# A gated attention kernel whose 264 steps run in an order written out by hand: another order, with the same instructions

## The reference

```
x = x + tanh(g_x) * xattn(layernorm(x), ctx, ctx)
x = x + tanh(g_f) * ffn(layernorm(x))
xattn: f_q, f_k, f_v = layer_norm(t) @ w_in.T, 8 heads of 128
       mixed = cw * cos(f_q, f_k) + vw * cos * decorr_scale + ww * q_ratio x k_ratio
       out = (mixed @ f_v) @ w_out.T + b_out
ffn:   q, k, v = x @ Wq, x @ Wk, x @ Wv, 16 heads of 16
       attn[key, query] = softmax over the queries of (q . k) / 16; z[query] = sum over keys of attn * v
       z = l2norm(z @ Wo); z = l2norm(z @ Wff); gelu(z)
```

## Time and profile before

| | us |
|---|---|
| three runs, median | 1335.22 (1333.38 to 1335.81) |
| profiled execution, own time | 1331.52 |
| its span, first to last instruction | 1329.8 |
| PE busy | 1197.1 (90%) |
| DVE busy | 1116.6 (84%) |
| ACT busy | 1012.5 (76%) |
| POOL busy | 206.9 (16%) |

### The profile page before, as it was taken

The page is one execution under the profiler, slowest core; times in us unless marked ns, Lnnn a source line. Parts: engine busy times, 40 slices in busy tenths (PEclk is TensorE's granted clock), DMA queues, the critical chain, the costliest instruction groups (busy, mean ns, idle before and its releaser), DMA issues. The chain is left out here.

```text
span 1329.8 us, 34850 instructions
## 1 busy us (share of the span) xinstructions
PE 1197.1 (90%) x10386; PEld 744.4 (56%) x10386; DVE 1116.6 (84%) x3180; ACT 1012.5 (76%) x3333; POOL 206.9 (16%) x160
## 2 busy tenths in 40 slices
PE   4999967999999999999989899989898999898965
PEld 2677536565646464656565656565555656564531
DVE  5986546798989898989898898989898989898964
ACT  5667113487979797979797979797888888888887
POOL 1443101202020202011110202020202020202000
PEclk9999879999999999999999999999999999999987
DMA  8450024463627281818181818182727254544650
GB/s 257 136 166 20 3 53 80 132 124 111 158 92 176 74 194 50 218 47 220 45 204 51 204 52 208 42 213 52 200 68 194 74 182 85 170 98 142 112 159 17
DMA packets 247888, 162.30 MB, mean 122 GB/s; under 512 B 94538, under 2 KB 235559, under 8 KB 247848
## 3 DMA queue, kind: packets, MB, share of 16 engines
q1 hardware_dynamic: 247848, 161.80, 46.3%
HBM read 86.74 MB, written 42.58 MB: 97 GB/s over the span
## 5 line engine op out<-in xcount | busy, mean ns | idle before, releaser
L1529 ACT ACTIVATE prob<-score,nm 128x256 f32<-128x256 f32 x1024 | 474.9, 485 | 61.4 <-DVE nm L1722 34.0
L1722 DVE TENSOR_REDUCE nm<-score 128x2 f32<-128x512 f32 x512 | 337.3, 681 | 17.2 <-PE score L1433 16.0
L1529 ACT ACTIVATION_READ_ACCUMULATOR prob<-score,nm 128x1 f32 x1024 | 222.5, 217 | 0.0
L1444 PE MATMUL attended<-prob,vsp 128*32 128x256 f32 x2048 | 134.9, 392 | 8.5 <-DVE vsp L1737 7.6
L1433 PE MATMUL score<-qstack,kstack 64*128 64x256 f16 x1024 | 97.0, 277 | 38.6 <-DMA kstack<-parts 27.4
L1642 DVE BATCH_NORM_STATS2 qst<-work 128x6 f32<-128x128 f32 x512 | 112.0, 284 | 22.3 <-PE work L895 22.3
L1588 POOL TENSOR_TENSOR l2r<-l2v,mhalf 128x4 f32<-128x4 f32 x16 | 16.1, 1009 | 599.0 <-DVE l2v L1694 599.0
L893 PE MATMUL work<-wTh,xTh 128*128 128x512 f16 x256 | 98.3, 384 | 5.4 <-DVE xTl L1636 3.5
L894 PE MATMUL work<-wTl,xTh 128*128 128x512 f16 x256 | 98.0, 383 | 0.0
L895 PE MATMUL work<-wTh,xTl 128*128 128x512 f16 x256 | 97.8, 382 | 0.0
L893 PE MATMUL work<-Vph,mTh 128*128 128x256 f16 (+1 forms) x320 | 87.4, 273 | 5.7 <-issue 4.8
(11 more groups left out here) (326 smaller groups left out, 3244.3 us busy)
## 6 DMA issues: line engine op xcount, KB each, us to landing
qstack<-parts SPq DMA_DIRECT2D x64, 256.0 KB, 3.8
kstack<-parts SPq DMA_DIRECT2D x64, 256.0 KB, 4.3
sqE<-sq_rows SPq DMA_DIRECT2D x64, 154.0 KB
s_xin<-in_x SPq DMA_DIRECT2D x8, 1024.0 KB, 6.0
xin<-in_x SPq DMA_DIRECT2D x16, 512.0 KB, 4.2
x2S<-in_x SPq DMA_DIRECT2D x16, 512.0 KB, 3.6
parts<-qh SPq DMA_DIRECT2D x32, 256.0 KB, 2.5
parts<-ql SPq DMA_DIRECT2D x32, 256.0 KB, 2.7
```

The source lines that it names most:

```text
L1444: last = nc.tensor.matmul(pvb[32 * j:32 * j + 32, t, :], vsp[:, k, (4 * e + j) * 2 * FD:(4 * e + j + 1) * 2 * FD], prob[:, n % PG, e, j, : ...
L1529: nc.scalar.activation(prob[:, g % PG, e, j + jj, :], sc[n % SC][:, jj * NQ:(jj + 1) * NQ], ACT.Exp, bias=nm[:, u + jj:u + jj + 1], accum_ ...
L1722: nc.vector.tensor_reduce(nm[:, u:u + 2], sc[n % SC][:, :].rearrange("p (u q) -> p u q", q=NQ), AX.X, ALU.max, negate=True).then_inc(max_r ...
```

## The change

All steps keep their instructions. `ORDER`, `HEAD`, `TAIL` and `MOVED` are replaced; the loop, the steps' code and the number of turns stay. The list of a turn begins elsewhere: `a0`, `a1`, `aux`, `qs2`, `rk`, `G1.h`, `G1.l`, `X1` and `M2` now stand at the end of the turn ahead of the one in which they stood, `back1` and `back2` with them. The bank of each chunk follows from its new place. In the order after, y0 is place 19 of the chunks (counted from 0), d5 place 16.

```diff
 ORDER = """
-G0 X1 G1.h M2 G2.l G0.h qs2 G3 G3.h ldx S2 M3 G1.l G0.l G3.l a0 X2 a0.v res V3 V5 pv1 V3.h M4 V5.h aux back1 M5 V3.l
-V0 X3 rk X4 V5.l z back2 pv1.v R0 S3 V4 V0.h fk0 V4.h X5 P0 M6 S4 X6 M7 V0.l V4.l fk0.h X7 sqe0 V2 M8 sqe1 fk0.l M9
-V2.h fk1 V2.l R1 X8 X9 S5 fk1.h vt1 a1 d0 M10 M11 X10 fk1.l vt0 S6 M12 a1.h P1 a1.l fk2 X11 d0.o E0 S7 fk2.h m0.h M13
-d1 L0 d2 R2 P2 X12 fk2.l M14 m0.l M15 X13 X14 d3 X15 d1.o d2.o S8 m1.h M16 d4 R3 m2.h M17 S9 m1.l X16 m2.l d3.o wq ldy
-d5 X17 d4.o P3 E1 S10 zT0 M18 m3.h zT0.h m4.h M19 y0 X18 m3.l m4.l X19 d5.o m5.h M20 zT1 zT0.f zT1.h L1 m5.l M21 zT0.l
-S11 y0.o M22 y1 X20 zT1.f M23 R4 zT1.l y1.o X21 X22 ln1 O0 X23 R5 back3 O1 q0 S12 S13 P4 O0. P5 lpow q0.o M24 M25 M26
-O1. M27 q1 q2 ln2 q1.o q3 X24 q2.o q3.o zz0 X25 X26 X27 S14 S15 M28 zz1 zz0.h zz0.l E2 zz1.h q4 X28 M29 q5 zz1.l q4.o
-M30 pk0 X29 X30 q6 q5.o M31 X31 pq0 pk0.h L2 R6 pq0.h R7 pk0.l P6 q6.o P7 q7 pq0.l E3 L3 O2 q7.o O2. O3 G5 qs1 pq1 O3.
-G5.h G5.l F1 F2 parts0 pq1.h V1 V1.h back0 pk1 S0 pq1.l G4 V1.l F3 M0 pk1.h pk1.l G4.h G4.l G1 M1 parts1 X0 F4 pv0
-pv0.v qpow G2 S1 G2.h out
+a1.l ldx pv1 V2 pv1.v M3 G4.l V2.h S2 sqe0 M4 M5 X2 V4 V4.h V5 V2.l G3 V4.l sqe1 V5.h V5.l X3 G3.h S3 R0 M6 G0 G3.l X4
+M7 G0.h X5 V3 G0.l fk1 S4 X6 z M8 X7 P0 fk1.h R1 d0 fk1.l P1 M9 S5 V3.h X8 V3.l V0 d0.o M10 X9 m0.h S6 M11 fk2 M12 E0
+V0.h fk2.h m0.l V0.l X10 X11 d1 fk2.l d1.o wq d2 X12 M13 d2.o L0 S7 m1.h R2 M14 X13 d3 vt0 fk0 X14 m1.l m2.h M15 d4
+vt1 S8 d3.o fk0.h m2.l X15 res m3.h M16 R3 P2 d5 X16 P3 M17 X17 fk0.l zT0 m3.l d4.o d5.o zT0.h S9 m4.h S10 M18 E1 m5.h
+m4.l L1 M19 m5.l back3 zT1 ldy zT0.f X18 y0 X19 M20 zT0.l zT1.h M21 zT1.f S11 X20 y1 X21 M22 M23 zT1.l X22 y0.o R4 O0
+X23 y1.o ln1 O1 O0. S12 R5 S13 O1. M24 P4 lpow P5 q0 q1 X24 E2 M25 M26 ln2 q2 q0.o zz0 X25 M27 X26 q1.o S14 X27 S15
+zz0.h zz1 q2.o q3 zz1.h M28 zz0.l zz1.l q4 R6 M29 X28 pq0 q3.o X29 M30 q4.o pk0 pq0.h M31 pq0.l pq1 X30 L2 q5 pk0.h P6
+pk0.l X31 R7 pq1.h P7 q5.o q6 E3 pq1.l q7 L3 O2 q6.o parts0 O3 rk q7.o pk1 O2. O3. V1 qs1 pk1.h G2 pk1.l F1 F2 V1.h
+back0 G2.h V1.l S0 pv0 G2.l F3 pv0.v G5 back2 G1 S1 M0 qpow parts1 M1 G1.h G5.h back1 G4 G5.l G1.l qs2 a0 X0 a0.v a1
+a1.h F4 aux G4.h M2 out X1
 """.split()
 
 HEAD = """
-ldx fk0 fk1 fk0.h fk1.h +ldy fk1.l z fk2 fk2.h fk2.l zT0 zT0.h zT1 zT0.f zT0.l zT1.h fk0.l zT1.f zT1.l q0 q1 q2 q0.o
+fk1 ldx fk1.h fk0 fk1.l z fk2 fk2.h fk0.h fk0.l zT0 zT0.h zT0.f zT1 fk2.l zT1.h zT0.l zT1.f zT1.l q0 q1 q0.o rk q1.o
...
 TAIL = """
...
-X30 E2 X31 pk0.h L2 R7 pq0.h P6 pk0.l pq0.l P7 E3 L3 O2 parts0 O2. O3 back0 O3. pq1 pk1 pq1.h pq1.l F1 pk1.h F2 S0 F3
+P5 S15 M29 zz0.h zz1.h E2 zz0.l zz1.l L2 M30 X28 X29 X30 pq0 M31 R6 X31 pq0.h R7 pk0 pq0.l P6 P7 pk0.h pq1 pk0.l E3 L3
+pq1.h O2 pq1.l parts0 O3 O2. O3. F1 pk1 back0 S0 pk1.h pk1.l parts1 F2 M0 F3 F4 S1 X0 back2 pv0 M1 back1 pv0.v out M2
...
-MOVED = {step: n for n, steps in {0: "G1 G2 G2.h G4 G4.h G4.l G5 G5.h G5.l V1 V1.h V1.l qpow qs1", 1: "M0 M1 S0 S1 X0", 2: "back1 back2 back3 pv1 pv1.v res"}.items() for step in steps.split()}
+MOVED = {step: n for n, steps in {0: "G1 G1.h G1.l G2 G2.h G2.l G4 G4.h G5 G5.h G5.l V1 V1.h V1.l a0 a0.v a1 a1.h aux qpow qs1 qs2 rk", 1: "M0 M1 M2 S0 S1 X0 X1", 2: "back3 pv1 pv1.v res"}.items() for step in steps.split()}
```

More of the change, by code:

```diff
@@ L965 @@
[L965 to L969, removed]
@@ L970 @@
-+q1.o +lpow +q2 +ln2 +q3 +zz0 +zz0.h +q2.o +q3.o +zz0.l +zz1 +q4 +zz1.h +zz1.l +q5 +q4.o +pk0 +q5.o +pq0 +pk0.h +pq0.h
-+q6 +pk0.l +pq0.l +q6.o +q7 +q7.o +pq1 +pq1.h +parts0 +G5 +back0 +pq1.l +G5.h +G4 +V1 +V1.h +G5.l +qs1 +qpow +G4.h
-+pk1 +G4.l +G2 +pk1.h +S0 +V1.l +G2.h +pk1.l +pv0 +M0 +X0 +parts1 +S1 +M1 +G1 +pv0.v
+fk1 ldx fk1.h fk0 fk1.l z fk2 fk2.h fk0.h fk0.l zT0 zT0.h zT0.f zT1 fk2.l zT1.h zT0.l zT1.f zT1.l q0 q1 q0.o rk q1.o
+q2 q2.o q3 q3.o q4 q4.o q5 q5.o q6 q7 V1 q6.o q7.o qs1 V1.h G2 G2.h V1.l G2.l qpow +ldx G5 G1 G1.h G5.h G5.l G1.l G4
@@ new lines @@
+a1 a1.h G4.h qs2 a0 a0.v +a1.l aux +V2 +V2.h +G4.l +V4 +V2.l +V5 +V4.h +G3 +V4.l +G0 +V5.h +G3.h +G0.h +G0.l +G3.l
++V5.l +fk1 +d0 +z +wq +sqe0 +V3 +sqe1 +fk1.h +V3.h +V3.l +V0 +d0.o +m0.h +m0.l +fk1.l +V0.h +V0.l +d1 +fk2 +d2 +fk2.h
++fk2.l +d1.o +m1.h +d2.o +d3 +m2.h +fk0 +fk0.h +d4 +m1.l +m2.l +vt1 +d3.o +m3.h +fk0.l +d5 +zT0 +d4.o +m3.l +zT0.h
++d5.o +m4.h +zT0.f +zT1 +zT0.l +vt0 +zT1.h +ldy +zT1.f +m5.h +y0 +m4.l +m5.l +y1 +zT1.l +y0.o +y1.o +q0 +ln1 +lpow
++q0.o +q1 +q2 +q1.o +ln2 +q2.o +zz0 +zz0.h +zz1 +zz1.h +q3 +zz0.l +zz1.l +q3.o +q4 +pq0 +q4.o +pk0 +pq0.h +pk0.h
@@ L973 @@
++pq0.l +rk +pq1 +pk0.l +pq1.h +q5 +pq1.l +parts0 +back0 +q6 +q5.o +q7 +q6.o +G2 +q7.o +pk1 +pk1.h +V1 +V1.h +qs1 +G2.h
++G2.l +G1 +G1.h +V1.l +S0 +pk1.l +back2 +G5 +parts1 +S1 +G1.l +M0 +qpow +G5.h +X0 +a1 +G5.l +qs2 +pv0 +M1 +a0 +pv0.v
++a1.h +G4 +a0.v +aux +X1 +M2 +back1 +G4.h
 """.split()
 TAIL = """
-qs2 G2.l G0 G1.h back2 X1 G0.h G3 G3.h G1.l M2 M3 a0 a0.v S2 G0.l V3 G3.l V5 pv1 M4 X2 X3 V3.h V3.l aux M5 V5.h X4 V0
-V5.l S3 pv1.v V4 V0.h back1 R0 rk M6 V0.l res X5 S4 M7 V4.h X6 X7 P0 V4.l V2 sqe0 a1 V2.h M8 M9 X8 V2.l R1 S5 d0 sqe1
@@ L982 @@
[L982 to L986, removed]
+res pv1 a1.l pv1.v V2 S2 V2.h M3 sqe0 G4.l V4 M4 V2.l G3 V5 X2 X3 M5 V4.h S3 X4 R0 P0 V4.l G0 V5.h M6 sqe1 G3.h X5
@@ new lines @@
+V5.l S4 V3 X6 G0.h G3.l M7 X7 V3.h M8 ldy M9 G0.l X8 R1 S5 M10 X9 d0 V3.l M11 X10 d0.o S6 V0 d1 m0.h X11 P1 M12 S7 M13
+m0.l R2 V0.h V0.l E0 d1.o d2 wq d3 X12 m1.h M14 X13 S8 d2.o m1.l L0 M15 P2 d4 d3.o X14 m2.h M16 M17 X15 R3 m3.h m2.l
+d5 vt1 X16 vt0 m3.l P3 X17 E1 S9 d4.o m4.h d5.o S10 M18 y0 X18 back3 m5.h M19 M20 M21 X19 m4.l X20 X21 L1 S11 m5.l R4
+M22 y1 X22 S12 M23 y0.o X23 O0 P4 y1.o M24 ln1 O0. lpow M25 X24 O1 S13 M26 O1. X25 ln2 X26 S14 zz0 M27 X27 R5 zz1 M28
+P5 S15 M29 zz0.h zz1.h E2 zz0.l zz1.l L2 M30 X28 X29 X30 pq0 M31 R6 X31 pq0.h R7 pk0 pq0.l P6 P7 pk0.h pq1 pk0.l E3 L3
@@ new lines @@
+pq1.h O2 pq1.l parts0 O3 O2. O3. F1 pk1 back0 S0 pk1.h pk1.l parts1 F2 M0 F3 F4 S1 X0 back2 pv0 M1 back1 pv0.v out M2
+X1 +M3 +pv1 +S2 +M4 +X2 +X3 +pv1.v +M5 +S3 +M6 +R0 +M7 +X4 +P0 +X5 +X6 +S4 +X7 +M8 +M9 +S5 +R1 +X8 +M10 +X9 +X10 +M11
++P1 +S6 +M12 +E0 +M13 +L0 +X11 +S7 +R2 +X12 +P2 +X13 +S8 +M14 +M15 +X14 +M16 +M17 +X15 +S9 +R3 +X16 +M18 +M19 +X17
++X18 +P3 +S10 +M20 +X19 +res +S11 +X20 +E1 +M21 +R4 +M22 +M23 +L1 +back3 +X21 +S12 +X22 +P4 +M24 +X23 +X24 +S13 +M25
++X25 +M26 +O0 +S14 +R5 +M27 +M28 +M29 +X26 +X27 +P5 +E2 +S15 +M30 +L2 +X28 +R6 +X29 +O1 +X30 +M31 +X31 +R7 +P6 +O0.
@@ L987 @@
++P7 +E3 +L3 +O2 +O1. +O2. +O3 +O3. +F1 +F2 +F3 +F4 +out
 """.split()
-MOVED = {step: n for n, steps in {0: "G1 G2 G2.h G4 G4.h G4.l G5 G5.h G5.l V1 V1.h V1.l qpow qs1", 1: "M0 M1 S0 S1 X0", 2: "back1 back2 back3 pv1 pv1.v res"}.items() for step in steps.split()}
+MOVED = {step: n for n, steps in {0: "G1 G1.h G1.l G2 G2.h G2.l G4 G4.h G5 G5.h G5.l V1 V1.h V1.l a0 a0.v a1 a1.h aux qpow qs1 qs2 rk", 1: "M0 M1 M2 S0 S1 X0 X1", 2: "back3 pv1 pv1.v res"}.items() for step in steps.split()}
 CHUNKS = [s for s in ORDER if any(t.startswith(s + ".") for t in ORDER)]
```

## The result

The median of four runs is **1348.04 us** (1347.02 to 1349.10), beside 1334.56 for the kernel before on the same chip: the ratio is 1.0101, 95% interval 1.0083 to 1.0118. The change makes the kernel slower by 13.5 us, 1%. The profiled execution took 1348.43 us with a span of 1346.7, 16.9 more than the profiled one of the kernel before. The two profiles lie further apart than the medians because the profiled execution before, 1331.52 us, was faster than each of the four timed ones (1333.38 to 1335.81), while the one after lies at its median.

The account below looks back on a forecast made before the run. The loop was taken as near TensorE's and VectorE's limits, losing time mostly at the seam. 8.45 + 27.3 + 0.1 + 32.4, plus 1.2 and 0.2, gave 69.6 us a turn, +13 us in fourteen: 1348 us, range 1324 to 1372.

Parts of the forecast that it names:

- The 3.7 us added from the profile before to the median before: Last step of the total: the runs' median lies 3.7 us above the profiled execution, so 1344.5 became 1348 us.
- Transfers: At the seam of two turns: S0's wait under 1 us, z's gone; worth at most some 2.5 us a turn.
- The chain of 8.45 us over GpSimd: At the seam, O3., nrs, rq: qs2 can start 8.45 us after TensorE leaves O3; 2.5 us lost there.
- 27.3 us of VectorE from qs2 to d5.o: VectorE's hand-counted work from qs2 through d5.o, for which y0 waits: 27.3 us a turn.
- 1.2 of waits: VectorE's waits inside its stretch from qs2 to d5.o: 1.2 us a turn, between 0 and 3 possible.
- those foreseen at V4.l and G0.l: Within VectorE's stretch: V4.l waits 0.5 us for X2 and V4.h, G0.l 0.4 for X4.
- d5.o to y0: Step from VectorE's d5.o to TensorE's y0, which takes d5's work bank: 0.1 us in the sum.
- 32.4 us from y0 to O3's end: TensorE's part of the turn: today's 27.5 us, y0 and S11 3.6, and pq1 1.3, together 32.4 us.
- The sum: Length of the new turn: floor 68.2 us, plus 1.2 and 0.2 of waits and gaps, 69.6 us, 0.9 more than 68.7.
- the 4 us allowed for them: HEAD and TAIL, the loop's two ends, taken as zero together, between -4 and +4 us.
- the clear gain: Rival, chance 0.13: the seam's chain is shorter than read, waits come off; 2.3 us a turn less, 1303 us.
- Late transposes: Rival, chance 0.12: transposes after V0.l come late, y0 waits 3.7 us more, 1399 us; if half, 1373.

## Why the prediction was right, and where not

The forecast was 1348, slower by 12.8 us of median; it came out slower by 13.5. The turn was forecast rightly, and its mechanism too in the main, but that the total fits so closely is partly luck. The forecast for an execution like the profiled one was 1344.5; that one took 1348.43, and 4.1 us of this is the lower clock of three turns, which no term held. The 3.7 us added from the profile before to the median before made this good, since the profile after did not lie below its median.

- **Transfers.** S0's wait and z's are gone, as said, and back1 kept aux, out and ldx waiting without a reader noticing. Their worth was put at 2.5 us a turn at most. In the four orders tried from the kernel before, taking the wait for kstack off or freeing what lay beside it gained nothing. That the chain out of nrs and ScalarE's row lie under the same wait fits the waits that took its place, but no run frees all of them, so this cause is argued and not shown.
- **The chain of 8.45 us over GpSimd** measured 8.46. Right in size, wrong in standing: it is not the one bound of the seam but one of two equal ones. Had rq been cheap, the forecast's own sum would have promised 1.4 to 2.5 us a turn, and the run gave none. The step that I left out is ScalarE's row. It did not move the number, as it ended with the other. O3., pk1.h, V1.h, G2.h, table load, F3, pv0.v, G1.h and G5.h, table load, X0, a0.v, a1.h lie end to end, and from kh to wqTh they last 8.5 us.
- **27.3 us of VectorE from qs2 to d5.o, and 1.2 of waits.** Measured from aux at 607.32 to the last md tile's end near 635.4: 28.1 us, 0.4 less than the two together. Inside it only 0.6 us of waits appear (0.17 at a score bank, 0.44 at R0); those foreseen at V4.l and G0.l do not. F4 and M2 were counted as a piece of the path; they run beside the round trip a0, a0.v, a1.h to a1.l and end together with it.
- **d5.o to y0.** The forecast had 0.1 us. zT1 stands between, waits for d4.o's bank, and y0 starts 0.5 us behind the last md tile (rows below): the 0.4 that the stretch was shorter came back here, two misses that cancel by luck.
- **32.4 us from y0 to O3's end** measured 32.46 (635.94 to 668.40).
- **The sum** was 69.6 us a turn and an ordinary one is 69.54. The forecast had +0.9 in all fourteen turns and nothing at the ends; it was +0.84, plus 4.1 us of lower clock, +2.6 in the head and -0.7 in the tail. The ends lie inside the 4 us allowed for them; the clock was in no term.

```profile
634.24 1.26 DVE L1677 SCALAR_TENSOR_TENSOR md<-work,rkc,sqE 128x256 f32<-128x256 f32 x3
```

```profile
635.16 0.66 PE L1343 MATMUL work<-ident,norm 128*128 128x128 f32 x4
635.94 0.27 PE L893 MATMUL work<-Vph,mTh 128*128 128x256 f16 x1
```

Of the rivals, the clear gain failed at its own ground: waits for transfers were not what cost the time. Late transposes fell as argued. Away from the sqE copies the first pair was issued in 1.43 and 1.50 us, at the pace of the second (1.33 and 1.52), and y0 found Vp ready; SyncE's timeline after:

```profile
612.67 5.37 SPq L1272 DMA_DIRECT2D sqE<-sq_rows  x12
625.91 1.43 SPq L1280 DMA_TRANSPOSE Vph<-VTh  x1
627.40 1.50 SPq L1280 DMA_TRANSPOSE Vpl<-VTl  x1
```

What stays open: whether VectorE's stretch from a1.l to d5.o sets y0, which the sum of the terms supports and no run shows alone, and whether an order with both ways to a1.l short exists without leaving work out. The head's 2.6 us are explained only in part. They are not yet there at the first y0 (225.28 us against 225.09 before); the second lies 1.5 us later (286.86 against 285.38), and the last matmul of the loop's first O3, which now has pq1 ahead of it, starts 2.3 us later (319.11 against 316.77).
